# Attention rows turned behind the next row's scores, weights split in strips, activation tables asked for sooner

## The reference

```python
# tokenizer: patches of 16 samples with a mask of ones
hid = silu(einsum('bnd,dm->bnm', xm, W_h) + b_h)       # 32 -> 1024
h   = einsum('bnm,mh->bnh', hid, W_o) + b_o + xm @ W_r + b_r
# attention without weights, 16 heads of 16, on the layernormed row
xc  = xh - mean(xh, tokens)
h   = h + softmax(xc @ xc.T) @ xh
# two layers on the layernormed rows
q, k, v = split(shift_token(x) @ wqkv); q, k = rotary(l2norm(q)*qs), rotary(l2norm(k)*ks)
x = x + local_attention(q, k, v) @ wo                  # 8 heads of 64, window 128
a, g = split(layernorm(shift_token(x)) @ w1 + b1)
x = x + (a * gelu(g)) @ w2 + b2
out = h + x
```

## Time and profile before

| | us |
|---|---|
| median of 3 runs | 2766.34 (2763.4 to 2767.32) |
| the profiled execution, its own time | 2766.27 |
| span of its profile | 2764.5 |
| PE busy | 2641.3 (96%) |
| DVE busy | 1918.9 (69%) |
| ACT busy | 1719.4 (62%) |
| POOL busy | 1399.9 (51%) |

### The profile page before, as it was taken

How to read it: one execution, slowest core, us unless ns; L and a number is a source line. 1 busy time by engine, 2 the same in 40 slices (tenths; PEclk the granted TensorE clock), 3 DMA queues, 4 the chain that set the end, 5 groups by cost and what they waited for, 6 DMA issues and landing times.

```text
span 2764.5 us, 67543 instructions
## 1 busy us (share of the span) xinstructions
PE 2641.3 (96%) x23040; PEld 2257.0 (82%) x23040; DVE 1918.9 (69%) x3771; ACT 1719.4 (62%) x4181; POOL 1399.9 (51%) x1466
## 2 busy tenths in 40 slices
PE   6999999858999999997999998999999999999998
PEld 4888888747888888886888886788888887788887
DVE  5777777547777777776655555777777777666664
ACT  3666666536777778775444444778777777444442
POOL 7888888658666666663100005866666666000000
PEclk9999999979999999999999999999999999999999
DMA  1111111111111111112211111111111111122221
GB/s 31 32 38 35 36 35 35 53 56 48 40 40 39 37 38 40 39 34 77 65 56 50 57 48 39 49 37 40 40 37 37 40 40 52 60 80 79 79 72 46
DMA packets 165603, 130.23 MB, mean 47 GB/s; under 512 B 23239, under 2 KB 163689, under 8 KB 165462
## 3 DMA queue, kind: packets, MB, share of 16 engines
q1 hardware_dynamic: 163157, 119.80, 14.0%
q0 software_dynamic: 2304, 8.47, 1.0%
HBM read 77.47 MB, written 50.33 MB: 46 GB/s over the span
## 4 chain that ended last, share of the span: by engine, by line
PE 70%; POOL 2%; SPq 2%; DVE 2%; issue 1%; DMA 1%; ACT 0%; POOLq 0%; DVEq 0%
PE const_banks L1291 6%; PE const_banks L1292 6%; PE const_banks L1293 6%; PE const_banks L1302 6%; PE const_banks L1304 6%; PE const_banks L1303 6%; PE const_banks L1389 5%; PE const_banks L1371 4%; PE const_banks L1399 4%; PE const_banks L1357 4%; PE const_banks L1418 3%; PE const_banks L1419 3%; PE const_banks L1420 3%; PE const_banks L1346 2%; PE const_banks L1344 2%; PE const_banks L1345 2%
## 5 line engine op out<-in xcount | busy, mean ns | idle before, releaser
L1019 ACT ACTIVATE attn_E<-const_banks,attn_nbias,attn_rn 128x128 f32<-128x128 f32 x1024 | 454.9, 485 | 8.6 <-DVE attn_nbias L1185 8.5
L958 POOL TENSOR_TENSOR attn_rn<-attn_ssm,const_neg_half 128x8 f32<-128x8 f32 x128 | 211.1, 1650 | 413.8 <-DVE attn_ssm L1201 313.6
L939 POOL TENSOR_TENSOR ffn_rstd<-ffn_var,const_neg_half 128x4 f32<-128x4 f32 x32 | 32.3, 1010 | 678.5 <-DVE ffn_var L1118 678.5
L952 POOL TENSOR_TENSOR attn_qk<-attn_rot_a,attn_rot_b 128x1024 f32<-128x1024 f32 x128 | 305.8, 2389 | 66.2 <-issue 55.6
L1180 DVE TENSOR_REDUCE attn_neg_top<-const_banks 128x8 f32<-128x1024 f32 x128 | 156.8, 1225 | 233.9 <-PE const_banks L1389 233.9
L1302 PE MATMUL const_banks<-weights_w_hi,attn_xT_hi 128*128 128x512 f32 x768 | 315.9, 411 | 2.6 <-ACT attn_sq L1059 2.4
L1304 PE MATMUL const_banks<-weights_w_hi,attn_xT_lo 128*128 128x512 f32 x768 | 304.6, 397 | 0.0
L1303 PE MATMUL const_banks<-weights_w_lo,attn_xT_hi 128*128 128x512 f32 x768 | 303.4, 395 | 0.0
L1217 DVE SCALAR_TENSOR_TENSOR ffn_gated<-const_banks,weights_b_col,ffn_gate 128x512 f32<-128x512 f32 (+1 forms) x192 | 143.7, 748 | 215.0 <-ACT ffn_gate L1086 207.8
L1291 PE MATMUL const_banks<-ffn_xT_hi,ffn_w_hi 128*128 128x512 f32 x704 | 282.4, 401 | 6.9 <-DVE ffn_xT_lo L1130 5.4
L1293 PE MATMUL const_banks<-ffn_xT_hi,ffn_w_lo 128*128 128x512 f32 x704 | 279.3, 397 | 0.0
(11 more groups left out here) (171 smaller groups left out, 7929.6 us busy)
## 6 DMA issues: line engine op xcount, KB each, us to landing
attn_x_res<-xa SPq DMA_DIRECT2D x128, 128.0 KB, 4.7
xb<-attn_x_new SPq DMA_DIRECT2D x128, 128.0 KB, 1.7
ffn_x_<-xb SPq DMA_DIRECT2D x32, 512.0 KB
h<-ident_h SPq DMA_DIRECT2D x64, 128.0 KB, 1.7
xa<-ident_n SPq DMA_DIRECT2D x64, 128.0 KB, 1.7
attn_x_<-xa SPq DMA_DIRECT2D x128, 64.0 KB
xa<-ffn_x_new SPq DMA_DIRECT2D x16, 512.0 KB, 3.4
ffn_add<-h SPq DMA_DIRECT2D x16, 512.0 KB, 6.9
```

Source lines behind the costliest of these rows:

```text
L952: pool.tensor_tensor(qk[:, slot].rearrange("p a n -> p (a n)"), rot_a[:].rearrange("p a h d -> p (a h d)"), rot_b[:].rearrange("p a h d -> ...
L958: pool.tensor_tensor(rn[:, slot, HEADS:], ssm[:, HEADS:], c["neg_half"][:, HEADS:], ALU.pow).then_inc(s["rn_done"], 1)
L1019: last = act.activation(E[:, r, i], ps_s[:, r, i * P:(i + 1) * P], ACT.Exp, bias=nbias[:, r, i:i + 1], scale=rn[:, slot, h:h + 1], accum_o ...
```

## The change

1. PE: the four transposes of TURN stand right behind the scores of the step instead of at its end. The lags DONE and STORE are one less, so the pipeline has 14 steps of depth instead of 15, and the written-out head of SP, ACT and DVE is 16 steps instead of 24.
2. POOL: its steps are all written out. The `idle` operation is gone. The weights of layer 0's attention are no longer loaded and split whole in the drain: `attention_part` issues the transfers at steps 12, 27 and 42 and splits 128 columns in each of the steps 14 to 25, 29 to 40 and 44 to 51. PE waits for `a_low` instead of `a_split` in layer 0.
3. ACT: an activation of one column with Exp at the start of layer 1's attention, and one with Gelu at step 68 of each attention, load the tables there.

```diff
-    OUT, STAT, CENT, SCORE, WEIGH, TURN, DONE, STORE = 8, 9, 10, 11, 12, 13, 14, 15
+    OUT, STAT, CENT, SCORE, WEIGH, TURN, DONE, STORE = 8, 9, 10, 11, 12, 13, 13, 14
...
                     need(pool, h_ps, 8 * i + u // 4 * 4 - 8)
-                    pool.tensor_tensor(idle[:], zero[:], zero[:], ALU.add)
                     pool.tensor_copy(hid_hi[:, slot, k], hid[:, half]).then_inc(hi_done, 1)
...
-                    if isinstance(t, int) and t in (ROWS + 5, ROWS + 7, ROWS + 9):
-                        piece = (t - ROWS - 5) // 2
-                        weights.load_attention(pool, 0, piece)
-                        weights.split_attention(pool, 0, piece)
-
-                run_eights(pool, ROWS, STORE, body)
+                    weights.attention_part(pool, t)
+
+                run_eights(pool, ROWS, STORE, body, loop=False)
...
                         last.then_inc(s["S_ps"], 1)
+                    if on(TURN):
+
+                        b = t - TURN
+                        need(pe, s["outT_ready"], b + 1)
+                        need(pe, s["att_done"], b)
+                        for j in range(4):
+                            last = pe.transpose(ps_out[:, 4 * j:4 * j + 4].rearrange("p h d -> p (h d)"), outT[:, j],
+                                                c["ident"][:])
+                        last.then_inc(s["out_ps"], 1)
                     if on(CENT):
...
                         last.then_inc(s["outT_ps"], 1)
-                    if on(TURN):
...
+    def attention_part(self, pool, t):
+
+        for piece, first, parts in ((0, 14, 12), (1, 29, 12), (KD, 44, KI * D // P)):
+            if t == first - 2:
+                need(pool, self.a_low, self.parts)
+                self.load_attention(pool, 0, piece)
+            if first <= t < first + parts:
+                if t == first:
+                    pool.wait_ge(self.loaded, 16 * self.loads)
+                if piece < KD:
+                    hi, lo = self.w_hi[:, piece], self.w_lo[:, piece]
+                else:
+                    hi, lo = [x[:].rearrange("p k n -> p (k n)") for x in (self.wo_hi, self.wo_lo)]
+                cols = slice((t - first) * P, (t - first + 1) * P)
+                pool.tensor_copy(hi[:, cols], self.stage[:, cols]).then_inc(self.a_high, 1)
+                self.parts += 1
+                pool.wait_ge(self.a_high, self.parts)
+                pool.tensor_tensor(lo[:, cols], self.stage[:, cols], hi[:, cols].bitcast(F32), ALU.subtract
+                                   ).then_inc(self.a_low, 1)
...
                 step = t - L if isinstance(t, int) else None
+                if step == 0 and layer:
+                    act.activation(ask[:], c["neg_half"][:, 0:1], ACT.Exp)
                 if step == ROWS + 3:
...
+                if step == ROWS + 4:
+                    act.activation(ask[:], c["neg_half"][:, 0:1], ACT.Gelu)
...
                     if step == 1:
-                        pe.wait_ge(w.a_split, 2 * w.PIECES * (layer + 1))
+                        if layer == 0:
+                            pe.wait_ge(w.a_low, w.parts)
+                        else:
+                            pe.wait_ge(w.a_split, 2 * w.PIECES)
```

More of the change, by code:

```diff
@@ L132, in front @@
         h = m.sb("h", [P, 8, D])
-        idle = m.sb("idle", [P, 1])
         n = Memory(nc, ctx, "ident")
@@ L429, in body @@
                         need(dve, s["h2_done"], b - 1)
-                        dve.tensor_tensor(att[:, u % 2], ps_out[:, :, 0:IHD],
+                        dve.tensor_tensor(att[:, (u - DONE) % 2], ps_out[:, :, 0:IHD],
                                           rsum[:].unsqueeze(2).to_broadcast([P, IH, IHD]), ALU.mult
@@ L699, in __init__ @@
         self.a_split, self.f_split = m.sem("a_split"), m.sem("f_split")
+        self.a_high, self.a_low, self.parts = m.sem("a_high"), m.sem("a_low"), 0
         self.loads, self.clears = 0, 0
@@ L762, in split_attention @@
             hi, lo = [x[:].rearrange("p k n -> p (k n)") for x in (self.wo_hi, self.wo_lo)]
-        n = 2 * (self.PIECES * layer + piece)
+        n = 2 * piece
         split(pool, hi, lo, self.stage[:, 0:KI * D if piece == KD else 3 * INNER], self.a_split, n)
@@ L804, in layers @@
         x_new = m.sb("x_new", [P, 2, D])
+        ask = m.sb("ask", [P, 1])
         banks = c["banks"]
```

## The result

| | before | changed |
|---|---|---|
| median of 4 runs | 2764.87 | 2738.51 (2735.05 to 2740.46) |
| ratio, 95% interval | | 0.9903 (0.9886 to 0.992) |
| the profiled execution, its span | 2766.27, 2764.5 | 2740.46, 2738.7 |

Two more sets of runs of the changed kernel gave ratios of 0.9908 and 0.9894.

A forecast was written before the change was run, and what follows sets the result against it. PE's order was taken to bound full steps (busy 416.74 of 417 us), waits the drain. Turn 3.9, fourth steps 3.2, drain 11.8 and tables 0.2 sum to 19.1: 2766.3 - 19.1 = 2747.2 us, range 2741 to 2758.

The forecast's parts named there:

- the turn's move: PE's turn behind the scores: 0.07 less in each of 56 steps, 3.9 us in all.
- The fourth steps: Every fourth step, when DVE also splits the input: earlier scores remove a wait of 0.27, 3.2 us over twelve steps.
- Exps as the next bound: Full steps on PE: the scores can't start earlier than 2.54 behind the shift matmuls, because of the exps.
- Strips: POOL's 32 pairs on 128 columns: 0.8 each, hidden in its 0.97 wait for the division, so no cost.
- Rival C: POOL becomes the bound: strips of 1.9 lengthen 32 steps by about 0.9, 29 us, giving 2776; chance 2%.
- The drain: Steps draining the pipeline: without the weight stalls and with a shorter last-row chain, 11.8 us less.
- Tables: ACT's table loads for Exp and Gelu, asked for while idle: 0.2 us less in all, bounds 0 and 0.6.
- A: Only the drain gains and full steps keep their length: 2754; chance 22%.
- B: Scores wait 0.2 for the exps in each of 56 steps, losing 11 us: 2765, no change; chance 5%.
- D: The table loads lie on the path: three of 1.28 go whole, 3.8 instead of 0.2, 2743.6; chance 4%.
- E: The moved weights don't help: only some 4 of the drain's 12 us go, 2755; chance 3%.
- The layers: Layers 0 and 1 after the front stage: of equal length as before.

The follow-up runs named there:

- turn_back: The changed kernel with the turn back at the end of PE's step and the old lags: 2750.61 us, ratio 0.994 to the kernel before.
- back_idle: turn_back with the one-column operation put back on POOL too: 2757.53 us in a single run.
- turn_only: The kernel before with only the turn moved, the lags and the index of `att` changed: 2754.55 us, ratio 0.9949.
- turn_inside: The changed kernel with the turn's transposes between the two halves of the scores: 2780.92 us, ratio 1.0051 to the kernel before.
- pieces_early: The changed kernel with the row's matmuls cut at 3 and 5 instead of 4 and 6: 2733.01 us, ratio 0.9873 to the kernel before.
- strips_twice: The changed kernel with each strip's cast and subtraction done twice: 2753.91 us, ratio 0.9948 to the kernel before.

## Why the prediction was wrong

**The step that failed is the turn's move**, "Sum 2.63 against 2.70: 0.07 less". Up to the centring's start the intervals were 1.09, 1.10 and 0.50, sum 2.69: each within 0.03 of its estimate, but the gain there only 0.01. What I left out is the end of the centring: having drawn it as a fixed block, I didn't ask what it follows. Its 0.91 to the next matmul became 0.81, as it no longer follows the scores' 32-row tiles. The other 0.08 of a step lie outside of these blocks, where I had put nothing: with the turn in its old place turn_back and back_idle show 0.07 of it as the dropped one-column operation's, which I had counted only as room for POOL; turn_only, which keeps the operation, gains 0.14 in these blocks and 0.04 outside. In all a step lost 0.19, not 0.07. My bounds were -8 to +3 for this term; with the fourth steps' 3.2 that is at most 11.2, and turn_only gave 12.0 of *full*.

**The fourth steps.** The 8.19 are gone, as said, and for the reason said: they stay with the turn in its old place (turn_back) and come back as 8.63 to 8.69 when the scores end later (turn_inside). In their place stand 7.72 to 7.75 without a strip, which is as long as the others, and up to 7.90 with one; that makes some 2.5 of the 3.2. The full part as a whole: 7.1 predicted, 12.1 measured. These 5.0 are most of the 7.3 that were missing; the rest is 0.5 in drain and tail, 0.9 in the layers, and under 1 us in the start and between the profiles and the medians.

**Exps as the next bound.** Right: the scores start 2.53 to 2.55 behind the shift in 44 of the 56 full steps (2.60 to 2.72 in the others, half of them fourth steps), and pieces_early, which loosens that, gains the 0.07.

**Strips.** 0.77 each, predicted 0.8. In sum they cost close to nothing, as predicted (some 0.8 us, in the fourth steps), but the room that I gave them was too wide: in their step POOL no longer waits for the division, where I had expected it to wait still. Rival C's sum was too dear: for the doubled strip of strips_twice, 1.67, it gives (1.67 - 0.97) x 32 = 22 us, and 13 were lost. The rule from the Trainium skill (SBUF — State Buffer, SBUF: two separate sides) agrees with rows of DVE's timeline in so far as a normalisation beside POOL's hidden cast, as at 202.54, takes up to twice its 0.41. But this is not the strips' doing: 25 of the 64 normalisations take 0.82 in the kernel before and 9 take 0.68 to 0.81 in the changed one, all of them beside a hidden cast and none beside a strip. No step shows a wait for it:

```profile
202.49 0.81 DVE L453 TENSOR_SCALAR ident_v<-tok_h,ident_mv,ident_rstd 128x256 f32<-128x256 f32 x1
```

**The drain.** 11.8 predicted; drain and tail together gained 12.3 between the first two profiles (81.4 to 69.1). The steps are 7.48 to 7.52 (7.6 assumed) and 6.78; the last row comes 16.3 behind the last scores (16 assumed). turn_back shows that it is the weights' part: 9.4 of the drain without the moved turn.

**Tables.** 0.2 predicted, none to be measured. The loads last 1.28 in every profile. The Trainium skill's price of 2.66 a switch (ScalarE: Activation LUTs, What ACT_TABLE_LOAD costs) would have given up to 8 us; leaving out both asks lost nothing that the medians show.

**Rivals.** A and B fall with the steps of 7.72 to 7.75, C with them too, D by the runs without asks, E with the drain of 43.6.

**The layers.** I let them stay as they were. Three profiles of the changed kernel show 2174.9, 2170.4 and 2169.5, two of before 2176.0 and 2178.3. Whether a us or two of that belongs to the change stays open; all 18 profiles taken cover 2168.9 to 2179.0.

## What to carry to other kernels

On a full engine, price a moved block by the start of the block *behind* its new and its old neighbours, not up to the next start: what an operation costs depends on the shape of what ran ahead of it. Putting blocks of one tile shape next to each other was worth more here (0.10 to 0.14 a step) than what I had read from the starts of the moved blocks (0.07). Before a helper engine is given work "in its wait", add up its chain in the busiest kind of step, and cut a first profile into stages before reading differences of a few us as effects.

## What I had not expected of the hardware

A group of the shape 128*128 is longer by 0.06 to 0.10 when it stands first behind groups of another shape, whichever it is (the centring 1.16 or 1.06, the transposes 0.66 or 0.60). And a one-column operation of 0.22 on POOL, with no wait in sight, lengthened PE's step from 7.85 to 7.92 with the turn in its old place, and hardly (7.72 to 7.75 without it, 7.74 to 7.76 with it) in its new one. Why is open.
